# A graph network on one core: edge units collected in pairs, and a sort whose ranks are added up by TensorE from a single layout of one-hots

## The reference

```python
x = _layernorm(x + _L0_gnn_ref(x, src, dst, W, b))          # mean of neighbours, linear
x = _layernorm(x + _L1_gnn_ref(x, edge_weight, src, dst))   # two weighted propagations
x = _layernorm(x + _L2_gnn_ref(x, edge_weight1, src, dst, W1, b1, W2, b2))
x = _layernorm(x + _L3_gnn_ref(x, edge_index, ...))         # two SAGE convolutions

# L2, the edge layer: a small network on every edge
x = concatenate([h[src], h[dst], e], axis=1)
m = relu(x @ W1 + b1) @ W2 + b2
h_new = segment_sum(m, dst, num_segments=N)
```

## Time and profile before

| | |
|---|---|
| median of 3 runs | 3848.96 us |
| profiled execution | 3849.64 us, of which the span is 3847.9 us |
| PE / DVE / ACT / POOL busy | 3315.3 / 2374.6 / 1334.1 / 943.1 us |
| build and first layer | 0 to 1240 us |
| weighted passes with the sort | 1240 to 2307 us |
| edge layer | 2307 to 3380 us |
| layer 3 | 3380 to 3848 us |
| mean granted TensorE clock | 0.943 of full |

### The profile page before, as it was taken

How to read it: one execution, slowest core, us unless ns; L and a number is a source line. 1 busy time by engine, 2 the same in 40 slices (tenths; PEclk the granted TensorE clock), 3 DMA queues, 4 the chain that set the end, 5 groups by cost and what they waited for, 6 DMA issues and landing times.

```text
span 3847.9 us, 141254 instructions
## 1 busy us (share of the span) xinstructions
PE 3315.3 (86%) x62784; PEld 3110.2 (81%) x62784; DVE 2374.6 (62%) x2669; ACT 1334.1 (35%) x2884; POOL 943.1 (25%) x905
## 2 busy tenths in 40 slices
PE   0668999999996888888888877898998899899998
PEld 0657999999996888887887776777787787789898
DVE  8986676676776988898999875334343343311122
ACT  0016777777772000000000004455455555400000
POOL 5588300000002454554555430000000000001100
PEclk9988999999996999999999988999999999999999
DMA  4316778787775788888777855555565565589797
GB/s 114 100 44 203 281 280 288 264 287 268 274 284 207 295 323 338 340 330 327 299 283 290 331 206 138 155 156 158 154 171 156 158 170 156 155 313 342 296 383 315
DMA packets 268515, 926.37 MB, mean 241 GB/s; under 512 B 96850, under 2 KB 161608, under 8 KB 229676
## 3 DMA queue, kind: packets, MB, share of 16 engines
q1 hardware_dynamic: 231608, 897.99, 65.7%
q0 software_dynamic: 14400, 14.77, 1.5%
q10 hardware_dynamic: 21912, 4.88, 0.6%
HBM read 666.80 MB, written 251.36 MB: 239 GB/s over the span
## 4 chain that ended last, share of the span: by engine, by line
issue 36%; PE 28%; DVE 22%; DVEq 5%; POOLq 4%; POOL 2%; DMA 1%; ACT 1%; SPq 0%; ACTq 0%
PE ps L1324 14%; PE ps L1297 6%; PE ps L1367 5%; DVE operand_room L2172 5%; DVE operand_room L2181 3%; DVE operand_room L2187 3%; DVEq L2189 3%; PE ps L1477 3%; DVE operand_room L542 2%; DVE operand_room L539 2%; POOL stream L846 2%; POOLq L525 1%; DVE junk L1651 1%; POOLq L527 1%; DMA a_counts<-stream 1%
## 5 line engine op out<-in xcount | busy, mean ns | idle before, releaser
L1324 PE MATMUL ps<-operand_room 64*128 64x50 bf16 (+1 forms) x18750 | 636.1, 221 | 40.6 <-DVE operand_room L1892 19.3
L1324 PEld LDWEIGHTS ps<-operand_room 64*128 64x128 bf16 x18750 | 614.0, 163 | 66.6 <-POOLq L531 15.2
L1372 PE MATMUL ps<-stream,node_room 125*64 125x125 f32 x10000 | 566.7, 273 | 11.0 <-DVEq L2074 6.7
L1372 PEld LDWEIGHTS ps<-stream,node_room 125*64 125x64 f32 x10000 | 543.1, 138 | 19.5 <-DVEq L2074 6.9
L1040 ACT CAST stream<-ps 128x500 bf16<-128x500 f32 (+2 forms) x700 | 431.3, 633 | 219.1 <-PE ps L1324 179.8
L1567 PE MATMUL ps<-stream 128*64 128x125 f32 x5000 | 445.2, 287 | 22.7 <-issue 20.7
L1040 ACT COPY stream<-ps 128x500 f32<-128x500 f32 (+2 forms) x700 | 422.2, 619 | 0.0
L1178 ACT ACTIVATE stream<-ps 128x320 f32<-128x320 f32 x500 | 219.6, 439 | 513.8 <-PE ps L1552 513.8
L1477 PE MATMUL ps<-operand_room 128*125 128x128 bf16 x3300 | 251.4, 241 | 157.4 <-DVEq L2189 157.4
L1477 PEld LDWEIGHTS ps<-operand_room 128*125 128x125 bf16 x3300 | 237.1, 156 | 175.6 <-DVEq L2189 169.9
L1549 PE MATMUL ps<-operand_room,stream 125*128 125x64 bf16 x5025 | 342.8, 195 | 39.3 <-issue 28.0
(11 more groups left out here) (289 smaller groups left out, 4971.4 us busy)
## 6 DMA issues: line engine op xcount, KB each, us to landing
stream<-a_weights SPq DMA_DIRECT2D x100, 3125.0 KB, 15.7
a_weights<-stream SPq DMA_DIRECT2D x500, 312.5 KB
stream<-a_counts SPq DMA_DIRECT2D x100, 1562.5 KB, 9.1
stream<-sorted_edges SPq DMA_DIRECT2D x67, 1400.0 KB
a_counts<-stream SPq DMA_DIRECT2D x500, 156.2 KB
node_room<-sorted_edges SPq DMA_DIRECT2D x33, 1400.0 KB
stream<-sorted_edges SPq DMA_DIRECT2D x67, 162.5 KB
node_room<-sorted_edges SPq DMA_DIRECT2D x33, 162.5 KB
```

Of the source, the lines that this page charges most:

```text
L1324: ins = pe.matmul(out if step == 0 else out[:, 1:2], low[s][rows_a, :, t], planes[s][rows_a, t // TI, what, :, t % TI], start=step == 0, s ...
L1372: ins = pe.matmul(ps_sum[SUM_BANK[MATRIX[k]][b]][half:half + D, 0:Q], tab_in_of(k)[0:Q, h, :], a[0:Q, h, :], start=h < 2, stop=h >= NPP - 2)
```

## The change

Edge layer: two units run one after the other, then two are collected (BATCH = 2), and the steps at which blocks are taken and multiplied move with it. Sort: `hot_pair` is gone; the base matmuls read `hot_src` column by column, 33 of 50 columns; the scan writes to a buffer of its own, `places`, which is multiplied with `hot_src`; PE sums its 50 rows through an identity (`sort_fold`), into bank 7 of PSUM; DVE copies the bases (`sort_bases`) and ranks out. `half_vals` is [5, 25, 34], so a tile's column is read every 34 elements. As bank 7 is used by the ranks, the last tile of L1B's product goes to `ps_t`, copied apart.

```diff
-    TAKE_STEP, PROD_STEP, NORM_STEP, ROOT_STEP, PARTS_STEP = 1, 3, 1, 2, 4
+    BATCH = 2
+    TAKE_STEP, PROD_STEP, NORM_STEP, ROOT_STEP, PARTS_STEP = 3, 6, 1, 3, 5
...
         half_vals = in_room(...)\
-            .rearrange("p (u i s t) -> p u i s t", i=VALS, s=HALF, t=2)
+            .rearrange("p (i s t) -> p i s t", i=VALS, s=HALF)
...
             def sort_base(b):
-                for u in range(TCOL):
-                    ins = pe.matmul(ps_base, later, hot_pair[b % 2][:, u].rearrange("p s t -> p (s t)"),
-                                    start=u == 0, stop=u == TCOL - 1)
+                for t in range(TILES):
+                    ins = pe.matmul(ps_base, later, hot_src[b % 2][:, :, 2 + t], start=t == 0, stop=t == TILES - 1)
                 ins.then_inc(base_ps, 1)
+
+            def sort_fold(b):
+
+                pe.wait_ge(places_rdy, b + 1)
+                if b:
+                    pe.wait_ge(rank_used, b)
+                for c in range(NPP):
+                    ins = pe.matmul(ps_rank, ident_b[:, :], places[:, c, 2:TPAD], start=c == 0, stop=c == NPP - 1)
+                ins.then_inc(rank_ps, 1)
...
             def sort_half(b, h):
-                    ins = pe.matmul(ps_half, half_vals[:, t // 2, :, :, t % 2].rearrange("p i s -> p (i s)"),
+                    ins = pe.matmul(ps_half, half_vals[:, :, :, t].rearrange("p i s -> p (i s)"),
                                     hot_rank[:, t // 2, :, t % 2], start=t == 0, stop=t == TILES - 1)
...
                     if n:
                         sort_half(s - 1, 1)
+                    if s < NPE:
+                        sort_fold(s)
                     if s + 1 < NPE:
                         sort_base(s + 1)
...
-                for w in range(UNITS + 1):
-                    if w < UNITS:
-                        unit(w)
-                    if w:
-                        collect_unit(w - 1)
+                for w in range(0, UNITS + BATCH, BATCH):
+                    for n in range(w, w + BATCH):
+                        if n < UNITS:
+                            unit(n)
+                    for n in range(w - BATCH, w):
+                        if n >= 0:
+                            collect_unit(n)
...
             def sort_pairs(b):
-                v.tensor_tensor(hot_pair[b % 2], high_iota.unsqueeze(1).to_broadcast(shape),
-                                key.unsqueeze(2).to_broadcast(shape), ALU.is_equal).then_inc(base_rdy, 1)
...
+            def sort_bases(b):
                 v.wait_ge(base_ps, b + 1)
-                    v.tensor_reduce(hot_src[b % 2][:, :, 1], ps_base.rearrange("p (s t) -> p s t", t=2), AX.X, ALU.add)\
-                     .then_inc(base_used, 1)
-                v.drain()
-                places = hot_src[b % 2].rearrange("p s t -> p (s t)")
-                v.tensor_tensor_scan(places, run_mask, places, 0.0, ALU.mult, ALU.add)
-                v.drain()
-                fold(v, b)
+                    v.tensor_copy(hot_src[b % 2][:, :, 1], ps_base).then_inc(base_used, 1)
+
+            def sort_counts(b):
+                v.drain()
+                v.tensor_tensor_scan(places.rearrange("p s t -> p (s t)"), run_mask,
+                                     hot_src[b % 2].rearrange("p s t -> p (s t)"), 0.0, ALU.mult, ALU.add)
+                v.drain()
+                v.tensor_tensor(places[:, :, 2:TPAD], places[:, :, 2:TPAD], hot_src[b % 2][:, :, 2:TPAD], ALU.mult)
+                v.drain()
+                v.sem_inc(places_rdy, 1)
 
             def sort_vals(b, h):
                 if h == 0:
+                    v.wait_ge(rank_ps, b + 1)
+                    v.tensor_copy(run_rank, ps_rank).then_inc(rank_used, 1)
...
             def sort_with(n):
                 s = n // 2
+                if n % 2 and s + 1 < NPE:
+                    sort_bases(s + 1)
                 if n % 2:
                     sort_vals(s, 0)
```

87 lines of the change are left out of this document (48 added, 39 removed).

## The result

The changed kernel takes 4533.11 us (median of 4 runs, 4517.1 to 4538.36), the kernel before 3841.39 (4 runs on the same chip, 3833.43 to 3854.41): ratio 1.1816, 95% interval 1.1772 to 1.1859 (estimated from the single runs; the two medians alone divide to 1.180). Forecast were 4470 us in a range of 4155 to 4640. The profiled execution has a span of 4532.0 us against 3847.9, 684.1 more.

The account below looks back on a forecast made before the run. PE and DVE were both near full in the weighted passes, PE alone bound the edge layer. 3850 us + 560 (sort on PE) + 105 (clock) - 45 (edge layer) = 4470 us, range 4155 to 4640.

Parts of the forecast that it names:

- The halves: Sort on PE: weight columns 68 bytes apart cost 227 ns a matmul, so a half takes 7.5 us instead of 2.05.
- The bases and the folds: Sort on PE, per period: strided base 3.05 us instead of 0.9 (ends 1.0 and 3.3), new fold 1.5 us.
- PE's idle time: Weighted passes: PE, busy 17.95 of 21.3 us a period, would fill the whole new period of 32.5 us.
- The clock: PE's clock falls in the slow halves, so each following product takes 1.3 us longer: +105 us, ends 0 and 155.
- The credit of 25 us: Weighted passes: about 25 us subtracted from 130, for products that the present waits already slow through the clock.
- The edge layer: Batches of two save 85 us of PE's tiling switches; part returns as pauses, so 45 saved, ends 0 and 85.
- DVE: Sort: DVE's work falls from 18.9 to 14.9 us a period; it waits for the bases at L2185, several hundred us.
- (a): Weighted passes: jumps cost 1.8 ns but PE's clock holds through the halves; total 4340 us, chance 0.28.
- low-price variant: Weighted passes: jump at 1.38 ns, half 5.75 us; total 4155 us with a held clock, 4260 without.
- (b): Sort on PE: a jump costs half as much, half 3.8 us, base 1.6; total 3925 us, chance 0.05.
- (c): Sort: PE reads strided columns without loss; period 20.3 us, total 3755 us with the edge layer, faster; chance 0.12.
- a base of 1 us beside halves of 7.5: Sort on PE: sign that only the stationary operand pays for jumps, -100 us on the sum.

## Why the prediction was right, and where its terms were off

The sign, the stage and the mechanism came out as forecast: the price of a line in PE's operand reads, and the clock behind it. Term by term:

- **The halves.** Forecast 227 ns a matmul and 7.5 us a half, measured 217 and 7.2; +545 us forecast, +490 measured. The price was right within 5%; what I subtracted was not: 2.04 us is a half at full clock, but part of the halves before ran slow, like the 3.78 us one in the earlier trace rows, and their mean was 2.51. The run with dense halves shows it from the other side, 232 us.
- **The bases and the folds.** +107 and +75 forecast, +105 and +81 measured. The base was the term without a row for its form, with 1.0 as the low end; it costs 3.2, and the run with dense bases shows that this is its own.
- **PE's idle time.** I let all 3.35 us a period go (167 us), 148 went by the windows, and 154 from the first product on.
- **The clock.** +105 forecast, at 1.3 us a product; the products take 1.64 more each, 164 us, with no credit to take off. This term was the most mis-sized, and 164 lies outside the ends of 0 and 155 that I gave it; the +2.1 us of my own row would have made an upper end of 210 - 25 = 185. The clock fell into the halves as expected, but does not return between them: fold and base run at the low level too, and the run with dense bases shows that they hold it down. The credit of 25 us for the waits before was wrong here, since those waits slowed halves rather than products: in the kernel before a fifth of the halves' loads start at the lower level and a fortieth of the products'. That the jumps don't notice the clock was right, 217 ns at either level.
- **Sum for the stage.** 665 forecast, 698 measured: halves -55, idle +19, products +34, the lost credit +25, fold +6, base -3, smaller matmuls +7. It is in part luck that the sum came so near: what the halves cost less hides nearly all of what the clock cost more. 7 us of the 698, and of the idle time's 19, lie ahead of the passes.
- **The edge layer.** -45 forecast, -12 measured (alone -9 in the total and +2 in its stage, both within what such runs scatter). The switching cost of 85 us was right: PE is busy 81 us less, and 87 us appear between the two kernels with small loads. The step that failed is taking the middle of 0 and 85: the other reading that the prediction itself gave, that something is fetched at its own pace there and a faster PE only waits longer, was nearly the whole truth: 69 of the 81 us came back as idle time. What PE waits for there is likely, and not shown, to be its instructions.
- **DVE.** 14.9 us a period forecast and 15.5 measured; the wait at L2185 of several hundred us is there (646), and costs little, as said.

Of the rivals, (a) with a held clock is what the run with more columns nearly makes real (PEclk 0.95), 4372 us on the scale of 3841 against its 4340. (Its low-price variant, 4155, which is also the low end of the range, leaves out the 25 us that 4340 takes off; with them it is 4130.) (b), half price for a jump, and (c), none, were refuted by the loads' 217 ns, though L1324, on which (b) rested, keeps its 62 ns a pair unexplained. But (c)'s reasoning was sound: without strided reads the new structure does gain (ratio 0.9807), its 3755 us is near the 3767 that this makes, and its period of 20.3 us near the 1017.8 / 50 = 20.4. What "a base of 1 us beside halves of 7.5" would have told did not occur.

## What to carry to other kernels

A layout that saves an engine's work is paid for by the engine that reads it: count the 16-byte lines that each matmul's two operands touch, not the elements (here 1.7 to 1.9 ns a line with all 128 rows in use), and look whether such a form already runs in the kernel at another price, as L1324 does. Then look at the granted clock, which fell here from 0.92 to 0.71 with the strided halves and stayed low beyond them, in fold, base and product. Keep the operands of the bounding engine dense, even for a second one-hot on an engine with slack. And where a busy engine pauses with no releaser, look at what the DMA engines carry at that time before making its work shorter.

## What was not expected of the hardware

- A weight load that touches 125 lines takes 217 ns at 1.2 and at 2.4 GHz alike, and the 50-column moving operand 93 ns at both, where the halves' dense matmuls go from 60 to 107 ns: the strided reads are not paced by TensorE's granted clock.
- 128 lines for 64 rows of the array (L1324) cost 62 ns for a pair of loads, far under that price; why is open.
- The granted clock falls in a stretch in which PE is never idle (0.92, then 0.50 in the half at 1723.58), and doubling the streamed columns of the halves, which is useless work, made the kernel 3.7% faster (1.1381 / 1.1816).
- The edge layer's broadcast loads cost PE 152 us of idle time in 1038 although nearly all of its pauses there name no releaser: it is idle 175 us with them and 23 with 64 of their 6400 columns. The clock, which is lower with these pauses, accounts for most of another 67 us.
